# Fifteen pairs of layer 3's output kept in SBUF, and TensorE's loop semaphores set back in mid-round

## The reference, cut to what matters

```python
x = coords @ fc0_w + fc0_b
x = transpose(x, (0, 3, 1, 2))
for sw, cw, cb in layers:                      # four
    x1 = spectral_conv(x, sw)                  # 20 x 20 modes of rfft2, mixed, irfft2
    x2 = einsum('bchw,oc->bohw', x, cw) + cb[None, :, None, None]
    x = gelu(x1 + x2)
x = transpose(x, (0, 2, 3, 1))
x = gelu(x @ fc1_w + fc1_b)
h = (x @ fc2_w + fc2_b)[..., 0]
h = h + attn(layernorm(h), W_Q, W_K, W_V)
h = h + ffn(layernorm(h), ...)
```

## Time and profile before

| | us |
|---|---|
| time before, median of 3 runs | 1543.83 (1543.54 to 1549.94) |
| profiled execution, its own time | 1545.64 |
| span of the profiled execution | 1543.9 |
| PE busy / DVE busy / ACT busy | 1375.7 / 1183.9 / 532.6 |
| layer 3's steps, conv of pair 4 to conv of pair 31 | 982.67 to 1134.15 of the span |
| head, first to last fc1 product | 1139.26 to about 1270 of the span |

### The profile page before, as it was taken

One profiled execution on the slowest core, in us unless ns is written; L12 is line 12 of the kernel. 1 busy time (PEld: TensorE's weight loads), 2 busy tenths in 40 slices (PEclk: granted clock), 3 DMA queues, 4 the chain that ended last, 5 costly groups with the idle time before them and its releaser, 6 DMA issues. The chain is left out here.

```text
span 1543.9 us, 69052 instructions
## 1 busy us (share of the span) xinstructions
PE 1375.7 (89%) x32216; PEld 708.4 (46%) x32216; DVE 1183.9 (77%) x1451; ACT 532.6 (34%) x673; POOL 92.4 (6%) x45
## 2 busy tenths in 40 slices
PE   9889989998999999889999998777779999989996
PEld 3444444445444444544444445444431118853332
DVE  4499999997999999789999997455510007878886
ACT  2422222223222222222222222333369993521221
POOL 1000000000000000000000000000000000036551
PEclk9999999999999999999999999999999998999998
DMA  6324242346666666566666663899997741056420
GB/s 229 114 113 166 112 166 113 139 166 224 248 247 245 249 241 254 181 250 246 248 249 243 251 235 144 321 374 373 375 384 282 269 177 59 8 126 155 116 76 14
DMA packets 59934, 315.80 MB, mean 205 GB/s; under 512 B 16704, under 2 KB 18688, under 8 KB 25984
## 3 DMA queue, kind: packets, MB, share of 16 engines
q1 hardware_dynamic: 36512, 177.95, 33.9%
q10 hardware_dynamic: 23264, 135.49, 21.5%
HBM read 176.05 MB, written 137.36 MB: 203 GB/s over the span
## 5 line engine op out<-in xcount | busy, mean ns | idle before, releaser
L909 ACT ACTIVATE act_c<-slots,conv_b 128x1024 f32<-128x1024 f32 x256 | 282.0, 1114 | 717.4 <-PE slots L580 717.2
L795 DVE STREAM_TRANSPOSE inv_out<-slots 128x1024 f32<-128x1024 f32 x256 | 304.7, 1229 | 97.2 <-PE slots L542 97.2
L580 PEld LDWEIGHTS slots<-inv_w,inv_out 64*64 64x64 f32 x16384 | 269.7, 135 | 197.9 <-issue 187.6
L580 PE MATMUL slots<-inv_w,inv_out 64*64 64x64 f32 x16384 | 300.8, 223 | 16.3 <-issue 11.2
L771 DVE STREAM_TRANSPOSE turned_h<-slots 128x1024 f32<-128x1024 f32 x200 | 237.9, 1228 | 21.7 <-PE slots L475 21.6
L475 PE MATMUL slots<-turned_w,fwd_w 32*64 32x512 f32 x3200 | 204.2, 604 | 27.6 <-DVE inv_out L795 21.7
L746 DVE STREAM_TRANSPOSE turned_w<-act_c 128x1024 f32<-128x1024 f32 x186 | 218.7, 1219 | 0.0
L542 PE MATMUL slots<-turned_k,inv_h 64*64 64x320 f32 x2048 | 169.2, 444 | 51.7 <-DVE turned_h L771 29.3
L564 PE MATMUL slots<-xin,conv_w 32*32 32x512 f32 x3072 | 112.2, 604 | 28.3 <-DMA xin<-act_scratch 18.9
L487 PE MATMUL slots<-turned_h,fwd_h 64*64 64x320 f32 x1600 | 132.9, 443 | 2.0 <-DVE turned_h L771 1.4
L542 PEld LDWEIGHTS slots<-turned_k,inv_h 64*64 64x64 f32 x2048 | 70.9, 133 | 129.6 <-DVE turned_h L771 75.5
(11 more groups left out here) (167 smaller groups left out, 1132.9 us busy)
## 6 DMA issues: line engine op xcount, KB each, us to landing
act_scratch<-act_c ACTq DMA_DIRECT2D x128, 1024.0 KB, 4.2
xin<-act_scratch SPq DMA_DIRECT2D x96, 1024.0 KB, 4.9
act_c<-act_scratch SPq DMA_DIRECT2D x32, 1024.0 KB, 5.8
mode_w<-in_sw_dram SPq DMA_DIRECT2D x20, 640.0 KB, 4.1
at_turned<-level_scratch SPq DMA_DIRECT2D x24, 256.0 KB, 4.3
at_ret_t<-level_scratch SPq DMA_DIRECT2D x20, 256.0 KB, 4.3
xin<-in_x_dram SPq DMA_DIRECT2D x4, 1024.0 KB, 8.5
turned_w<-in_x_turned_dram SPq DMA_DIRECT2D x3, 1024.0 KB, 5.0
```

Source lines behind the costliest of these rows:

```text
L580: mm = nc.tensor.matmul(banks[half * 64:(half + 1) * 64, 2 * two + odd, at:at + 64], inv_out[rows, t % 2, i, two, s, 2 * half:2 * half + 2 ...
L795: nc.vector.transpose(dst, src).then_inc(inv_turned, 1)
L909: nc.scalar.activation(act_c[:, t % RING, :, at, :].rearrange("p i q m -> p q i m"), banks[:, at, :].rearrange("p q (i m) -> p q i m", i=2 ...
```

## The change

Three things change.

1. **Eleven pairs of layer 3 stay in SBUF in spare space, and four more in `act_c`.** `KEPT` names pairs 1, 3, 5, 7, 9, 11, 15, 18, 21, 24 and 27. Their Gelu writes into buffers that layer 3 no longer needs (`turned_w`, `turned_h`, `mode_w`) or into parts of `modes` whose pairs have been read by then (`SPARE_FREE` names the pair whose `inverse_h` the Gelu waits for). The last four pairs, 28 to 31, stay in the four slots of `act_c`. None of these fifteen is stored or loaded; the other 17 (`STORED`) are, and take the slots of `act_c` in turn by their place among the stored.
2. **The head begins with the pairs that finished last.** `HEAD_ORDER` is 28, 29, 30, 31, 0, 1, ..., 27. So that the planes come out in the order of before, the images are rolled by eight on the host.
3. **The `nop`s of TensorE's loops move into the second step of the round.** In layers 1 and 2: two behind `inverse_h`, two behind `conv`, three behind `dft_w`, two left at the end. In layer 3: two behind `inverse_h`, three behind `conv`, none at the end. Their number is that of before.

```diff
@@ -43,6 +43,11 @@
...
 H_STORES = 8 * 16
+SPARE_FREE = [0, 0, 0, 0, 0, 9, 13, 17, 20, 23, 26]
+KEPT = [1, 3, 5, 7, 9, 11, 15, 18, 21, 24, 27]
+LAST = [PAIRS - RING + k for k in range(RING)]
+STORED = [t for t in range(PAIRS) if t not in KEPT + LAST]
+HEAD_ORDER = [(t + PAIRS - RING) % PAIRS for t in range(PAIRS)]
 FRONT_LOADS = 3 * 16
...
@@ -351,6 +356,23 @@
...
+        def after_last_store(i):
+            return 16 * ((LAYERS - 1) * (PAIRS // RING) + i // RING + 1)
+
+        def pair_of(space):
+            return space.rearrange("p (i q m) -> p i q m", i=2, q=4)
+
+        spare = [flat(turned_w[:, b]) for b in range(2)] + [flat(turned_h[:, b]) for b in range(2)]
+        spare += [flat(mode_w[:])[:, 0:2048], flat(front.normed)]
+        spare += [front.y_t[:, 0:2048], front.y_t[:, 2048:4096]]
+        spare += [flat(front.y2)[:, 0:2048], flat(front.y2)[:, 2048:4096], flat(front.weighted)[:, 0:2048]]
+
+        def last_home(t):
+
+            if t in KEPT:
+                return pair_of(spare[KEPT.index(t)])
+            return act_c[:, (STORED.index(t) if t in STORED else t) % RING]
+
...
@@ -389,14 +411,15 @@
...
-            def load_head(t):
-
-                if t >= RING:
-                    sp.wait_ge(fc1_done, 2 * (t - RING) + 2)
-                    sp.wait_ge(act_stored[t % RING], after_store(LAYERS - 1, t))
-                else:
-                    sp.wait_ge(act_stored[t % RING], after_store(LAYERS - 1, t + PAIRS - RING))
-                sp.dma_start(flat(act_c[:, t % RING]), act_dram[t]).then_inc(head_in[t % RING], 16)
+            def place_before(i):
+
+                return HEAD_ORDER.index(STORED[i - RING] if i >= RING else LAST[i])
+
+            def load_head(i):
+
+                sp.wait_ge(fc1_done, 2 * place_before(i) + 2)
+                sp.wait_ge(act_stored[i % RING], after_last_store(i))
+                sp.dma_start(flat(act_c[:, i % RING]), act_dram[STORED[i]]).then_inc(head_in[i % RING], 16)
...
@@ -456,9 +477,11 @@
...
-            def give_back(sem, count):
-
-                pe.nop().then_inc(sem, -count)
+            def give_back(*used):
+
+                for sem, count in used:
+                    pe.nop().then_inc(sem, -count)
+                    taken[sem.name] += count
...
@@ -593,6 +616,8 @@
...
                     inverse_h(l, j + 1)
+                if back:
+                    give_back((modes_turned, 2), (act_in[0], 16))
                 final = j == PAIRS - 1 and not last
...
@@ -601,11 +626,17 @@
...
                 conv(l, j)
+                if back:
+                    give_back((act_high, 2), (act_in[1], 16))
+                if back and last:
+                    give_back((inv_turned, 4))
                 inverse_w(l, j, 0)
...
                     dft_w(forward(l + 1, j - 2))
+                if back and not last:
+                    give_back((inv_turned, 4), (act_turned, 2), (w_turned, 4))
                 inverse_w(l, j, 1)
...
@@ -614,16 +645,14 @@
...
                 rounds = count // 2
-                used = [(act_high, 2), (inv_turned, 4), (modes_turned, 2), (act_in[0], 16), (act_in[1], 16)]
-                if l < LAYERS - 1:
-                    used += [(act_low, 2), (act_turned, 2), (w_turned, 4), (modes_set, 2)]
+                before = Counter(taken)
                 with pe.Fori(0, rounds):
-                    for j in range(first, first + 2):
-                        step(l, j)
-                    for sem, count in used:
-                        give_back(sem, count)
-                for sem, count in used:
-                    taken[sem.name] += count * rounds
+                    step(l, first)
+                    step(l, first + 1, back=True)
+                    if l < LAYERS - 1:
+                        give_back((act_low, 2), (modes_set, 2))
+                for name in taken:
+                    taken[name] = before[name] + (taken[name] - before[name]) * rounds
...
@@ -694,15 +723,17 @@
...
                 if n < IMAGES:
-                    if n % 2 == 0:
-                        pe.wait_ge(head_in[n // 2 % RING], 16 * (n // 2 // RING + 1))
+                    t = HEAD_ORDER[n // 2]
+                    if n % 2 == 0 and t in STORED:
+                        i = STORED.index(t)
+                        pe.wait_ge(head_in[i % RING], 16 * (i // RING + 1))
                     if n > 0:
...
                                 banks[u * HID:(u + 1) * HID, head_bank(n, a), :], w1[a * CH:(a + 1) * CH, :],
-                                act_c[a * CH:(a + 1) * CH, n // 2 % RING, n % 2, 2 * u:2 * u + 2, :].rearrange(
+                                last_home(t)[a * CH:(a + 1) * CH, n % 2, 2 * u:2 * u + 2, :].rearrange(
                                     "p b m -> p (b m)"), start=True, stop=True)
...
@@ -898,21 +929,34 @@
...
                 for t in range(PAIRS):
-                    if l > 0 or t >= RING:
+                    last = l == LAYERS - 1
+                    home = last_home(t) if last else act_c[:, t % RING]
+                    if last and t in KEPT:
+                        k = KEPT.index(t)
+                        act.wait_ge(inv_h_done, after_inverse(l, max(0, SPARE_FREE[k])))
+                    elif last:
+                        i = STORED.index(t) if t in STORED else None
+                        slot = t % RING if i is None else i % RING
+                        before = (i if i is not None else max(j for j in range(len(STORED)) if j % RING == slot) + RING)
+                        act.wait_ge(act_stored[slot], after_last_store(before) - 16)
+                        if before < RING:
+                            act.wait_ge(w_done, forward(l, before + PAIRS - RING) + 1)
+                    elif l > 0 or t >= RING:
                         before = (l, t - RING) if t >= RING else (l - 1, t + PAIRS - RING)
                         act.wait_ge(act_stored[t % RING], after_store(*before))
-                        if before[0] < LAYERS - 1:
-                            act.wait_ge(w_done, forward(before[0] + 1, before[1]) + 1)
+                        act.wait_ge(w_done, forward(before[0] + 1, before[1]) + 1)
                     for two in range(2):
...
                         act.wait_ge(summed, after_out(l, t, two))
-                        nc.scalar.activation(act_c[:, t % RING, :, at, :].rearrange("p i q m -> p q i m"),
+                        nc.scalar.activation(home[:, :, at, :].rearrange("p i q m -> p q i m"),
                                              banks[:, at, :].rearrange("p q (i m) -> p q i m", i=2), ACT.Gelu,
                                              bias=conv_b[:, l:l + 1]).then_inc(act_high if two else act_low, 1)
-                        if two == 0 and t == PAIRS - 1 and l < LAYERS - 1:
+                        if two == 0 and t == PAIRS - 1 and not last:
                             act.drain().then_inc(act_half, 1)
+                    if last and t not in STORED:
+                        continue
                     act.drain().then_inc(act_ready, 1)
-                    act.dma_start(act_dram[t], flat(act_c[:, t % RING])).then_inc(act_stored[t % RING], 16)
+                    act.dma_start(act_dram[t], flat(home)).then_inc(act_stored[(i if last else t) % RING], 16)
             for n in range(IMAGES):
```

19 lines of the change are left out of this document (9 added, 10 removed).

## The result

The changed kernel took 1521.61 us (median of 4 runs, 1518.87 to 1532.35) against 1543.68 (1541.79 to 1549.94) for the kernel before on the same chip: ratio 0.9862, 95% interval 0.9818 to 0.9906. On another chip, beside the experiments that compare with it, it took 1518.30 (6 runs, 1515.01 to 1525.10), ratio 0.9838 (0.9809 to 0.9868). It is 22 to 25 us faster; 31.9 were forecast. 1521.61 lies just inside the end of the range (1505 to 1522) and outside what the likeliest case gave itself (1508 to 1517). The profiled execution has a span of 1520.0 us, 23.9 less than before.

What follows compares the result with a forecast made beforehand. It took layer 3 as bound by DMA traffic of 2 MB a pair, layer 2's loop by DVE, the head by PE and ACT. Gains of 24.6 + 5.8 + 1.5 = 31.9 us gave 1512 us, range 1505 to 1522.

Steps and rivals of the forecast that it cites:

- the likeliest case: Whole kernel: the forecast by its own terms, 1512 us, from 1508 to 1517, given a chance of 0.68.
- What bounds the kernel, and the two floors: Layer 3: 2 MB a pair at 375 GB/s sets 5.59 us a pair; without the load's wait, 4.64.
- With a store beside every second load I expect the middle of 4.8 and 8.7, 6.75: just in time.: Layer 3's loads: landing in 6.75 us, within the 6.8 allowed; stretch 126.9 us, gain 24.6.
- The sign named for being wrong: Layer 3: conv still waiting for xin more than about 3 us in all would show the forecast wrong.
- loads still set layer 3's pace: Rival, layer 3: loads take 7.7 us, period 5.1, stretch 137.7, time 1523 us; chance 0.14.
- The dense pairs 12 to 17, 1.6 us: Layer 3, five stores in six pairs: up to 3 us late, half of it, 1.6, taken.
- The round's end: Layer 3: without nops there the 5.26 us step meets 4.64; stores gone alone would lose 8 us of the gain.
- Nops in mid-round cost 0: Moved nops, layers 1 to 3: cost 0; 3.5 us in layer 3 kept in range. Rival that they show: 0.08.
- Layers 1 and 2: Their loops: 8.41 us a pair instead of 8.52 with the nops moved, gain 5.8 us together.
- The boundary: Last conv of layer 3 to the head's third fc1 image: 8.74 us instead of 10.25, gain 1.5.
- Start of layer 3: Stall of 3.64 us in pair 2's products, 4.8 us lost: left in place, gain 0; rival that it vanishes 0.08.
- Slower, 0.02: Rival, layer 3's loop: the start's stall comes back there, 4.8 us each time, up to 1584 us; chance 0.02.

Runs made afterwards that it cites:

- e8: Kernel before with the nops moved and the load of xin waiting only for conv's last product, all 32 pairs of layer 3 stored and loaded: 1535.71 us.
- e3: Changed kernel without any store in layer 3, the head reading what layer 2 left in DRAM: 1503.64 us.
- e12: Changed kernel with layer 3's stores issued later, at conv plus 1.32 of the next pair instead of conv plus 0, loads where they were: 1513.66 us.
- e4: Changed kernel with the load of xin in all layers waiting for conv's last product, issued at conv plus 1.31 instead of 2.34: 1514.15 us.
- e5: Changed kernel with other pairs kept, so that stored pairs are spread more evenly, as many stores: 1517.50 us.
- e10: Changed kernel with the earlier load of e4 in layer 3's own loop alone: 1505.57 us.
- e11: e10 with the more evenly spread kept pairs of e5: 1508.14 us.
- e7: e4 with all nops at the end of a round as before: 1526.95 us.
- e1: Changed kernel with all nops at the round's end as before: 1529.32 us.
- e9: Changed kernel with layer 3's load waiting for the second half of inverse_w, issued at conv plus 3.3: 1533.94 us.
- e2: Kernel before with only the nops moved as in the change, all 32 pairs of layer 3 stored and loaded: 1537.33 us.

## Why the prediction was wrong

By its steps:

- **What bounds the kernel, and the two floors.** Right, but for the rate. 2 MB a pair bound layer 3 when all is stored (e8: engines full, 143 us even with early loads); 375 GB/s was what was moved and not the limit, so 5.31 a pair and not 5.59 is the bound by traffic. And a pair takes 4.62 when loads are in time (4.64 forecast; e3).
- **"With a store beside every second load I expect the middle of 4.8 and 8.7, 6.75: just in time."** This step failed. The term hung on it, 24.6 us, and 10.6 came. It holds two errors. The first: 6.75 is a mean, and 6.8 is a deadline that each load has to meet by itself. There are two slots of `xin`, so a load that is 2 us early gives nothing to the next. e12 shows this error nearly alone: its mean is 6.28, below the deadline, and yet 9 of 28 loads are over 6.9 us and the stretch is 4.5 over the floor. The second is larger: a load's time does not lie between 4.8 and 8.7 by the share of stores. Loads and stores as many as in e4 and e12 land with a mean of 7.25 in the changed kernel against 5.95 and 6.28 there, and a store takes 8.9 in place of 5.0 and 4.4. It depends on where in the period store and load are issued. At conv plus 0 and plus 2.34 some of the sixteen parts of each stay behind, late loads move the next store and load on, and that goes on for several pairs (the loads issued behind conv 12 to conv 17, for pairs 14 to 19: 8.1, 9.8, 9.7, 7.4, 8.1, 8.7 us). The sign named for being wrong, more than 3 us of waits for `xin`, came: 15.0.
- **The rival "loads still set layer 3's pace"**, given 0.14, is what happened, and its numbers were near: loads 7.7 (measured 7.25 mean, 7.54 median), stretch 137.7 (140.86), time 1523 (1521.6, with the 5.3 of layer 3's start in it). "Two slots of `xin` leave no reserve" stood there, and had to stand in the sum. Its price, too, was worked out from a mean, (2.5 + 7.7)/2 a step; from the mean that was measured, 7.25, it would be 4.87, 131.5 us for the stretch. Two steps cannot be shorter than 9.24 however early a load lands, so only the late loads count, and the stretch came to 140.86.
- **The dense pairs 12 to 17, 1.6 us.** The steps into pairs 13 to 18 took 4.95, 5.59, 6.64, 6.16, 5.24 and 5.32 in the changed kernel, 33.9, which is 6.2 over six of 4.62 (of the 6.16 some 1.5 is the lower clock, the load having landed 0.8 before). Spreading the pairs (e5) gained 0.5 us in all: with loads issued at the bad moment the late steps only move. With the earlier load, e10 and e11, it gained 1.8.
- **The round's end.** The working was right and its place in the order of causes was not: 7.7 us with loads in time (e4 against e7), nothing without (e1 against the changed kernel).
- **Nops in mid-round cost 0.** Right: `conv` in e4_early_load steps 4.62 at both kinds of step; five nops stand there too. The lead of 0.2 us at L580, which gave the bound of 3.5, did not cost anything behind conv. The rule of the Trainium skill that I weighed there, "TensorE: Matmul & The Clock Gate", "Architectural detail", a queue of 64, gave 0 as well; these runs agree with its result and don't show a depth.
- **Layers 1 and 2.** 5.4 for 5.8, at 8.41 a step nearly throughout, alike in all kernels with moved nops. The forecast's steps hold.
- **The boundary.** 8.55 for 8.74, gain 1.7 for 1.5.
- **Start of layer 3.** The stall fell from 3.64 to 1.06 us and 5.3 us came, where I had left 0 and given its end 0.08. Without the store of pair 1 it stays short: conv 2 to conv 3 is 6.20 to 6.63 us in seven such kernels, 7.17 to 7.91 in e1, e7 and e12, and 10.44, 10.41 and 9.95 in the three kernels that store pair 1. So the store has a part in it and is not alone: with the later load (e9), without that store, it is 9.35. What such a stall stands beside is in the last section.
- **Slower, 0.02**: no stall came into the loop.

That a store issued 2.3 us behind a load and as much ahead of the next is the bad moment, is shown by e4 and e12, which moved one or the other by a microsecond and got nearly the same cure. From a store to the next load are 1.3 us in e4, 1.0 in e12, 2.3 in the changed kernel and 3.3 in e9, and the stretches are 125.7, 129.3, 140.9 and 153.7; in e4 and e9 the deadline moved along with it, in e12 it did not, and 7.3 of e9's are steps at the lower clock. How e4's 15.2 us divide between the two is not measured apart; e12's 11.6 are the moment alone. Nor are the two distances told apart, from a load to the next store (2.3, in e4 3.3, in e12 3.6, in e9 1.3) and from that store to the next load: whatever lengthened one shortened the other. Why two of a transfer's sixteen parts stay behind then, stays open. That the next load is issued while the one before has 3.1 us to go (1.8 in e12) stands beside it, but was not tried by itself.

## What to carry to other kernels

A transfer into one of two slots has a deadline of its own: compare it with the late ones among the loads, not with a mean, and look at where each of them is issued within the period. When a stretch waits for loads and the DMA engines are not full (0.85 here), move the issue: with fifteen stores fewer, a microsecond in the wait that releases a load or a store was worth 11 to 15 us; with all stores left, and the engines full, 5.8 (e2 against e8). Neither stands for the other: the stores gave 8.0 with the loads at the bad moment (e2 against the changed kernel) and 17.4 with the earlier load (e8 against e4). And a cost that is hidden behind another bound, as the nops at the round's end, is to be priced at the order in which the bounds fall.
